# Row maxima eight slots ahead of the exponents in place of ten, in a fused attention and FFN kernel

## The chip, the cores and the metric

The kernel runs on one core of one Trainium2 chip. The metric is device time in microseconds (us), lower is better: before the change the median of 3 runs is 427.05 us (425.29 to 427.09).

## The reference

Input X has 8 batches of 512 rows of 256 numbers, float32. With xn the layernorm of X over the last axis, the result is X + attention(xn) + ffn(xn), float32:

```python
q, k, v = (split_heads(xn @ W.T) for W in (W_q, W_k, W_v))    # 16 heads of 16
q, k = rope(q), rope(k)
scores = causal(einsum("bhqd,bhkd->bhqk", q, k) * 16 ** -0.5) # upper triangle: lowest float
attention = merge_heads(softmax(scores) @ v) @ W_o.T

def fake_quant_fp8(t):                                        # one scale for the whole tensor
    scale = 448 / max(amax(abs(t)), 1e-12)
    return float8_e4m3(t * scale) / scale
ffn = fake_quant_fp8(xn) @ fake_quant_fp8(weight).T + bias
```

The scale of xn needs the largest absolute value of all eight batches.

## The kernel before

**Slots.** The five engines run five programs of their own, tied by semaphores. After a start-up part each program walks through the same numbered slots, from FIRST_SLOT = -LEAD - 1 up to 162. A batch takes 20 slots (SLOTS), 160 for the eight; a slot holds two banks (512 columns each in PSUM) of transposed scores with their exponents, for one fifth of a group of four heads. What is done in a slot is written in tables by hand: an offset per kind of work, relative to 20 times the batch's number. Within a slot each engine's program has a fixed order, and an engine never goes past an instruction that waits.

**Two kinds of scores.** The exponents need each row's maximum beforehand. So the scores are computed twice. `compare` (L989, PE) puts scores into one of three banks s_ps, two banks a slot, and `row_max` (L658, DVE) takes the maxima of each bank's rows. LEAD slots later `attend` (L970, PE) makes the transposed scores in two banks st_ps, with the maximum subtracted, and ACT's exponents (L818) read them. Slots below 0 have `compare` alone, the last LEAD slots of the 160 have `attend` alone. `scores(at, ahead)` interleaves the two, first on PE in each slot. `compare` waits until the bank three before it has been read by DVE, `attend` until the bank two before it has been read by ACT.

**How a maximum becomes a shift.** After ten banks a group's 16 columns of maxima are complete. `turn_max` ("mt", L1058, PE) waits for all of the group's maxima and transposes them into a shared bank; `split_max` (L691, L693, DVE) splits them in two float16 rows, negated; `shift_rows` (L398, SP) sends the two rows into q_st, where they are two more rows of the contraction. The first `attend` of a group waits for that landing.

**The shared banks.** Two PSUM banks, m_ps, serve all the other work of the loop: projections of q and k ("qk", L954, read by DVE's rope, L609 and L610), of V ("v", L1011, read by ACT's copy, L825), transposes of heads ("o", L1018, read by DVE's normalisation, L667 and L671), of two normalised blocks ("at", L1025, read by ACT's copy, L839), outputs ("fin", L1038 and L1046, read by DVE's `finish`, L679), "mt", two steps ("spread") that spread the quantisation's maxima over the partitions, and some filling matmuls ("busy", in five slots). `schedule()` sorts all these by slot, and within a slot by the order of OFFSETS; the bank alternates from item to item. Before each item `bank_free` lets PE wait until the reader of the item two places earlier is done:

```python
at = [i[1:] for i in SHARED].index(item)
if at >= 2:
    kind, n, k = SHARED[at - 2][1:]
    ...
        done, per = reader[kind]
        eng.wait_ge(done, per * n + k + 1)
```

In a slot PE does its scores, then turnings of batches (before slot 0), then the shared items, then PV matmuls (L1080: a first block at slots 3, 8, 13 and 18, the others at 6, 11, 16 and 21). DVE does the slot's two banks of maxima, then `weight_step`, then its part of the shared items in their order, then steps of the quantisation (L755, L759). ACT does its exponents and then copies, among them `copy_heads` (L832) of the first group, in slot 7, which waits for all four "o" of the batch before. In numbers within a batch of 20 slots the loop's items before the change are: 0 fin 1; 1 mt 1; 2 fin 2; 3 o 0; 4 o 1; 5 fin 3; 6 mt 2; 7 o 2, at 0; 8 o 3; 9 v 0; 10 qk 0; 11 mt 3; 12 qk 1; 13 at 1; 14 v 1; 15 qk 2; 16 mt 0 (of the next batch); 17 qk 3; 19 fin 0.

**The prelude.** Batches 0 and 1 are normalised and turned first, batch 0's q and k written to DRAM and read back stacked by heads. In slots -11 to -1 batches 2 to 7 are normalised by ACT (L773), turned by PE (`turn_rows`, L934) into two banks that the exponents and PV use from slot 0 on, and copied by ACT (L797), each at its TURN_SLOT; batch 1 is projected, its rope's result rotated (POOL), cast (ACT, L803) and split (POOL, L349), and V of batch 0 is projected in slots -2 and -1. Statistics of batches 6 and 7 come at slots -LEAD and -LEAD + 3 on DVE. From slot 0 PE waits until all batches are turned.

Of the kernel before, what the change touches and what calls it, by code (L numbers as in the profile page):

```python
# [22 lines left out]
HG = 4  # L23
NG = H // HG
SLOTS = 5 * NG
LEAD = 10
PAIR = 2 * T
SCALE = float(DH) ** -0.5
EPS = 1e-5
# [18 lines left out]
assert BANKS == 2 * SLOTS and ITEMS_UP_TO[-1] == ITEMS  # L48


OFFSETS = {("v", 0): -11, ("v", 1): -6, ("mt", 0): -4, ("mt", 1): 1, ("mt", 2): 6, ("mt", 3): 11,
           ("o", 0): 23, ("o", 1): 24, ("o", 2): 27, ("at", 0): 27, ("o", 3): 28, ("at", 1): 33,
           ("fin", 0): 39, ("fin", 1): 40, ("fin", 2): 42, ("fin", 3): 45,
           ("qk", 0): -30, ("qk", 1): -28, ("qk", 2): -25, ("qk", 3): -23}
LAST_FINS = {("fin", 0): 31, ("fin", 1): 32, ("fin", 2): 34, ("fin", 3): 35}
SPREAD = [(15, "spread", 0, 0), (17, "spread", 0, 1)]
EARLY = {("qk", 1, 0): -LEAD - 1, ("qk", 1, 1): -LEAD - 1, ("qk", 1, 2): -9, ("qk", 1, 3): -8, ("v", 0, 0): -2, ("v", 0, 1): -1}
CHAIN = {("rotate", 0): -27, ("high", 0): -24, ("low", 0): -23, ("write", 0): -21, ("rotate", 1): -21, ("high", 1): -19,
         ("low", 1): -18, ("write", 1): -16, ("read", 0, 0): -19, ("read", 0, 1): -15, ("read", 1, 0): -12,
         ("read", 1, 1): -7}  # L60
EARLY_CHAIN = {("rotate", 0): -10, ("high", 0): -9, ("low", 0): -8, ("write", 0): -7, ("rotate", 1): -7, ("high", 1): -6,
               ("low", 1): -5, ("write", 1): -4, ("read", 0, 0): -5, ("read", 0, 1): -1, ("read", 1, 0): 4,
               ("read", 1, 1): 5}
TURN_SLOT = {2: -10, 3: -8, 4: -7, 5: -6, 6: -4, 7: -3}
BUSY = {slot: 8 for slot in (0, 2, 4, 5, 7)}
LARGEST_SLOT = (0, 2, 4, 5, 7, 8, 9, 11)
DVE_STATS, ACT_STATS = (0, 1, 2, 3, 6, 7), (4, 5)
# [2 lines left out]
def schedule():  # L70


    order = {key: i for i, key in enumerate(OFFSETS)}
    items = [(EARLY.get((kind, n, k), SLOTS * n + (LAST_FINS[kind, k] if (kind, n) == ("fin", NB - 2) else off)),
              order[kind, k], kind, n, k)
             for (kind, k), off in OFFSETS.items() for n in range(NB) if (kind, n) != ("qk", 0)]
    items += [(slot, len(order), kind, n, k) for slot, kind, n, k in SPREAD]
    items += [(slot, len(order), "busy", slot, count) for slot, count in BUSY.items()]
# [4 lines left out]
SHARED_BANK = {item[1:]: i % 2 for i, item in enumerate(SHARED)}  # L83
FIRST_SLOT, END_SLOT = -LEAD - 1, SLOTS * NB + 3

# [9 lines left out]
def exponent_slot(slot):  # L95

    n, s = divmod(slot, SLOTS)
    return (n, s) if 0 <= n < NB else None


def maximum_slot(slot):

    return exponent_slot(slot + LEAD)

# [7 lines left out]
def chain_at(slot, *step):  # L112

    if slot == EARLY_CHAIN[step]:
        return 1
# [36 lines left out]
def attention_ffn_block(nc, x, wq, wk, wv, wo, wf, bias, cos, sin, out):  # L152
    with ExitStack() as ctx:
# [6 lines left out]
        def sem(name):  # L160
            return ctx.enter_context(nc.semaphore(name))
# [126 lines left out]
        wquant = sem("wquant")  # L288
# [168 lines left out]
        def _(eng):  # L457
# [15 lines left out]
            def invert(n):  # L473

                if n in ACT_STATS:
                    i = ACT_STATS.index(n)
                    eng.wait_ge(ln_square, NQ * (i + 1))
                    eng.tensor_scalar(ve[:, n, :], squares[:, i, :], 1.0 / D, EPS, ALU.mult, ALU.add).then_inc(ln_var, 1)
                    eng.wait_ge(ln_var, i + 1)
                else:  # L480
                    eng.wait_ge(ln_ve, 2 * (DVE_STATS.index(n) + 1))
                eng.tensor_tensor(rstd[:, n, :], ve[:, n, :], half[:, :], ALU.pow).then_inc(ln_rstd, 1)
                eng.wait_ge(ln_rstd, 2 * n + 1)
                eng.tensor_tensor(shift_x[:, n, :], nmean[:, n, :], rstd[:, n, :], ALU.mult).then_inc(ln_rstd, 1)  # L484
# [17 lines left out]
            def mask(n, s):  # L502

                u = s % 5
                if u < 2:
                    ap, pat = prob[u].rearrange("p (h q) -> p h q", h=2)[:, :, 0:P], [[0, 2], [1, P]]
                elif u < 4:
                    ap = prob[u].rearrange("p (h q) -> p h q", h=2)[:, :, 0:2 * P]
                    pat = [[0, 2], [0, 2], [1, P]]
                else:  # L510
                    ap, pat = prob[u].rearrange("p (h q) -> p h q", h=4)[:, :, 0:P], [[0, 4], [1, P]]
                eng.wait_ge(exp_done, HALVES * n + 2 * (s + 1))
                eng.sem_inc(mask_begun)
                eng.affine_select(out=ap, in_=ap, compare_op=ALU.is_ge, fill=0.0, base=0,  # L514
                                  pattern=pat, channel_multiplier=-1).then_inc(masked, 1)
# [23 lines left out]
            for slot in range(FIRST_SLOT, END_SLOT):  # L539
# [4 lines left out]
                if at is not None:  # L544
                    mask(*at)
                if slot == -LEAD - 1:
                    invert(4)
                    invert(5)
                if slot == -LEAD + 1:
                    invert(6)  # L550
                if slot == -LEAD + 4:
                    invert(7)
# [26 lines left out]
        def _(eng):  # L579
# [33 lines left out]
            def weight_step(s):  # L613

                nw = NC * D
                if s == 3:
                    eng.wait_ge(w_in, 16 * 4)
                    eng.tensor_reduce(amax[:, NB:NB + 1], wf_sb[:, :, :], AX.XY, ALU.max,
                                      apply_absolute_value=True).then_inc(amax_done, 1)
                if s == 13:  # L620
                    eng.wait_ge(amax_done, NB + 1)
                    eng.tensor_reduce(amax2[:, 0:1], amax[:, 0:NB], AX.X, ALU.max).then_inc(amax_done, 1)
                    eng.tensor_copy(amax2[:, 1:2], amax[:, NB:NB + 1]).then_inc(amax_done, 1)
                if s == 15:
                    eng.wait_ge(full["spread"], 1)
                    eng.tensor_reduce(amax_r[:, :], shared["spread", 0, 0][0:2, 0:P], AX.X, ALU.max).then_inc(wquant, 1)
                    eng.wait_ge(consts, 6)
                    eng.wait_ge(wquant, 1)
                    eng.tensor_tensor(amax_d[:, :], ident[0:2, 0:2], amax_r[:, 0:1].to_broadcast([2, 2]), ALU.mult)\
                       .then_inc(wquant, 1)  # L630
                if s == 17:
                    eng.wait_ge(full["spread"], 2)
                    eng.tensor_scalar(amax_b[:, :], shared["spread", 0, 1][:, 0:2], 1e-12, None, ALU.max)\
                       .then_inc(wquant, 1)
                    eng.wait_ge(wquant, 3)
                    eng.reciprocal(inv[:, :], amax_b[:, :]).then_inc(wquant, 1)
                    eng.tensor_scalar(unscale[:, :], shared["spread", 0, 1][:, 0:2], 1e-12, 1.0 / FP8_MAX, ALU.max, ALU.mult)\
                       .then_inc(wquant, 1)
                if s == 21:
                    eng.wait_ge(wf_scaled, 1)  # L640
                    eng.tensor_scalar(qe[:, 0:nw].bitcast(U32), qv[:, 0:nw].bitcast(U32), 0x7F800000, None,
                                      ALU.bitwise_and).then_inc(qw_exp, 1)
                    eng.wait_ge(qw_exp, 1)
                    eng.tensor_scalar(qe[:, 0:nw], qe[:, 0:nw], 2.0 ** -6, 1.5 * 2.0 ** 20, ALU.max, ALU.mult)\
                       .then_inc(wquant, 1)
# [94 lines left out]
            for slot in range(FIRST_SLOT, END_SLOT):  # L740
                at = maximum_slot(slot)
                if at is not None:
                    n, s = at
# [24 lines left out]
        def _(eng):  # L768
# [42 lines left out]
            def exp(n, s):  # L811
                g, u = divmod(s, 5)
                if n > 0 or g > 0:

                    eng.wait_ge(pv_done, 8 * n + 2 * (g - 1) + (1, 1, 2, 2, 2)[u])
                for half in range(2):
                    eng.wait_ge(st_full, 2 * (SLOTS * n + s) + half + 1)
                    eng.activation(prob[u][:, half * T:(half + 1) * T], st_ps[ST_BANK[2 * s + half]][:, :],  # L818
                                   ACT.Exp, scale=exp_scale[:, 0:1]).then_inc(exp_done, 1)
# [45 lines left out]
            for slot in range(FIRST_SLOT, END_SLOT):  # L865
# [12 lines left out]
                if at is not None:  # L878
                    exp(*at)
                for n in [n for n, at_slot in TURN_SLOT.items() if at_slot == slot]:  # L880
                    copy_turned(n)
# [38 lines left out]
        def _(eng):  # L920
# [172 lines left out]
            def bank_free(item):  # L1093

                kind, n, k = item
                at = [i[1:] for i in SHARED].index(item)
                if at >= 2:
                    kind, n, k = SHARED[at - 2][1:]
                    if kind == "spread":
                        eng.wait_ge(wquant, 1 + 2 * k)  # L1100
                    elif kind != "busy":
                        done, per = reader[kind]
                        eng.wait_ge(done, per * n + k + 1)
                else:
                    eng.wait_ge(roped, at + 1)
# [16 lines left out]
            for slot in range(FIRST_SLOT, END_SLOT):  # L1122
# [3 lines left out]
                scores(exponent_slot(slot), maximum_slot(slot))  # L1126
                for n in [n for n, at_slot in TURN_SLOT.items() if at_slot == slot]:
                    turn_rows(n)
# [61 lines left out]
```

## Time and profile before

| | |
|---|---|
| median of 3 runs | 427.05 us (425.29 to 427.09) |
| the profiled execution | 426.62 us, span 424.9 us |
| PE busy | 383.1 us, 90% of the span, 3034 matmuls |
| DVE busy | 356.4 us, 84% |
| ACT busy | 299.9 us, 71% |
| POOL busy | 247.3 us, 58% |
| mean granted clock of TensorE | 0.972 |
| HBM | 84 GB/s over the span |

Times in the profile's rows are microseconds from the start of the span, means of one instruction are nanoseconds. PE is TensorE's matmul and PEld its weight load, DVE VectorE, ACT ScalarE, POOL GpSimd, SP the engine that issues the transfers. L989 is line 989 of the kernel's file. A row of the timeline gives start, length, engine, line, operation, what is written and read, how many instructions are merged in it, and in brackets the engine's idle time before it with what ended it.

### The profile page before, as it was taken

What the parts mean: (1) busy time and instruction counts of PE and PEld (TensorE: products, weight loads), DVE (VectorE), ACT (ScalarE), POOL (GpSimd) and SP (SyncE); (2) the same over time, 40 slices, a digit from 0 to 9 for tenths busy, and PEclk for the clock granted to TensorE, in tenths of its full rate; (3) what the DMA queues carried; (4) which work ended last, traced back from release to release, by engine and by line L of the source; (5) the groups of instructions that cost most, each with busy time, mean ns of one, the idle gap of its engine ahead of it and who ended that gap; (6) DMA issues with size and microseconds to landing.
All of it is one profiled execution on the core that took longest, in us unless ns stands there. A gap on an engine that the chain in (4) does not pass through costs nothing.

```text
span 424.9 us, 9531 instructions
## 1 busy us (share of the span) xinstructions
PE 383.1 (90%) x3034; PEld 210.4 (50%) x3034; DVE 356.4 (84%) x1358; ACT 299.9 (71%) x507; POOL 247.3 (58%) x270
## 2 busy tenths in 40 slices
PE   7988799988788999899989998999899988896967
PEld 7675466644234545454445444544454443343436
DVE  3888849997889999799979997999799988898203
ACT  3698726665976878777867786778677768777651
POOL 6547402433578767576767567756864665247550
PEclk9998879999899999999999999999999999999988
DMA  7955233000540143314341235124510461101111
GB/s 269 328 156 99 64 89 77 1 3 2 137 117 12 39 134 91 90 39 121 90 104 39 93 97 127 38 59 130 127 39 32 122 161 40 50 2 54 52 50 49
DMA packets 27810, 36.40 MB, mean 86 GB/s; under 512 B 3984, under 2 KB 25872, under 8 KB 26320
## 3 DMA queue, kind: packets, MB, share of 16 engines
q1 hardware_dynamic: 27760, 35.79, 30.9%
q8 instruction: 24, 0.39, 0.4%
q14 instruction: 26, 0.21, 0.2%
HBM read 22.94 MB, written 12.58 MB: 84 GB/s over the span
## 4 chain that ended last, share of the span: by engine, by line
PE 64%; DVE 17%; ACT 8%; issue 8%; POOL 2%; DVEq 0%; ACTq 0%; POOLq 0%
PE o_ps L1080 13%; PE st_ps L970 10%; DVE scratch L658 8%; PE m_ps L1011 7%; PE m_ps L1038 7%; PE m_ps L954 7%; PE s_ps L989 6%; ACT prob L818 6%; DVE prod L610 3%; PE s_ps L926 3%; PE m_ps L926 2%; PE m_ps L1018 2%; PE m_ps L1046 1%; DVE prod L609 1%; PE m_ps L1058 1%
## 5 line engine op out<-in xcount | busy, mean ns | idle before, releaser
L818 ACT ACTIVATE prob<-st_ps,exp_scale 128x512 f32<-128x512 f32 x320 | 204.1, 688 | 81.0 <-PE st_ps L970 79.9
L658 DVE CUSTOM_DVE_ANT_0 scratch<-s_ps,causal 128x512 bf16<-128x512 f32 (+3 forms) x512 | 220.8, 482 | 26.8 <-PE s_ps L989 26.4
L514 POOL TENSOR_SCALAR_AFFINE_SELECT prob<-prob 128x512 f32<-128x512 f32 (+1 forms) x160 | 88.4, 554 | 141.0 <-ACT prob L818 140.2
L989 PE MATMUL s_ps<-k_st,q_st 48*128 48x512 f16 (+3 forms) x512 | 106.5, 303 | 11.1 <-DVE rowmax L658 10.5
L970 PE MATMUL st_ps<-q_st,k_st 50*128 50x128 f16 (+3 forms) x512 | 104.5, 300 | 10.8 <-ACT prob L818 9.1
L1080 PE MATMUL o_ps<-prob,v_sb 128*17 128x512 f32 (+3 forms) x1024 | 82.9, 442 | 7.8 <-ACT heads L832 5.1
L970 PEld LDWEIGHTS st_ps<-q_st,k_st 50*128 50x128 f16 x512 | 33.1, 94 | 88.5 <-ACT prob L818 66.4
L989 PEld LDWEIGHTS s_ps<-k_st,q_st 48*128 48x128 f16 x512 | 33.5, 94 | 27.4 <-DVE rowmax L658 17.7
L658 DVE DVE_READ_ACCUMULATOR2_ANT rowmax<- 128x1 f32 x512 | 40.6, 79 | 0.0
L1080 PEld LDWEIGHTS o_ps<-prob,v_sb 128*17 128x17 f32 x1024 | 23.3, 97 | 32.6 <-issue 19.0
L1011 PE MATMUL m_ps<-wv_sb,xnT 128*128 128x256 f32 x128 | 33.7, 408 | 0.0
L1038 PE MATMUL m_ps<-wo_sb,attnT 128*128 128x256 f32 x116 | 32.6, 403 | 0.0
L349 POOL TENSOR_TENSOR parts<-rot,parts 128x1024 f16<-128x1024 f32 x14 | 29.9, 2139 | 3.2 <-ACT parts L803 3.2
L1011 PEld LDWEIGHTS m_ps<-wv_sb,xnT 128*128 128x128 f32 x128 | 24.1, 198 | 6.8 <-issue 3.9
L832 ACT COPY heads<-o_ps 128x512 f32<-128x512 f32 x32 | 18.9, 590 | 11.2 <-PE m_ps L1018 8.0
L609 DVE SCALAR_TENSOR_TENSOR prod<-m_ps,qk_scale,cos_sb 128x512 f32<-128x512 f32 x30 | 22.3, 742 | 4.2 <-PE m_ps L954 3.2
L954 PE MATMUL m_ps<-x_parts,wk_parts 128*128 128x512 f32 x84 | 24.5, 429 | 0.0
L954 PE MATMUL m_ps<-x_parts,wq_parts 128*128 128x512 f32 x84 | 22.9, 410 | 0.7 <-issue 0.7
L1038 PEld LDWEIGHTS m_ps<-wo_sb,attnT 128*128 128x128 f32 x116 | 19.7, 189 | 7.4 <-issue 5.9
L773 ACT ACTIVATE xnT<-xnT,shift_x,rstd 128x256 f32<-128x256 f32 x32 | 16.5, 592 | 9.3 <-POOL shift_x L484 9.3
L1018 PE MATMUL m_ps<-ident,heads 128*128 128x128 f32 x116 | 19.4, 291 | 3.2 <-DVE attn L671 3.2
L610 DVE SCALAR_TENSOR_TENSOR prod<-m_ps,qk_scale,sin_sb 128x512 f32<-128x512 f32 x30 | 22.1, 736 | 0.0
(125 smaller groups left out, 510.0 us busy)
## 6 DMA issues: line engine op xcount, KB each, us to landing
qk_parts<-parts SPq DMA_DIRECT2D x14, 512.0 KB, 3.1
xnT<-x_dram SPq DMA_DIRECT2D x8, 512.0 KB, 9.0
x_res<-x_dram SPq DMA_DIRECT2D x8, 512.0 KB, 5.1
q_st<-qk_parts SPq DMA_DIRECT2D x15, 256.0 KB, 4.3
k_st<-qk_parts SPq DMA_DIRECT2D x15, 256.0 KB, 3.7
out_dram<-x_res SPq DMA_DIRECT2D x7, 512.0 KB, 3.7
q_st<-qk_parts SPq DMA_DIRECT2D x17, 128.0 KB, 3.8
k_st<-qk_parts SPq DMA_DIRECT2D x17, 128.0 KB, 4.3
```

The source lines that it names most:

```text
L349: eng.tensor_tensor(parts[:, w, 1, a:z, :], rot[:, w, a:z], parts[:, w, 0, a:z, :], ALU.subtract).then_inc(low_done[w], z - a)
L514: eng.affine_select(out=ap, in_=ap, compare_op=ALU.is_ge, fill=0.0, base=0, pattern=pat, channel_multiplier=-1).then_inc(masked, 1)
L610: eng.scalar_tensor_tensor(out=c, in0=bank[:, :], scalar=to_range, in1=sin_sb[:, :], op0=ALU.mult, op1=ALU.mult)\
L658: eng.tensor_tensor_reduce(scratch[:, at % 3, col:col + w], s_ps[at % 3][:, col:col + w], causal[:, T - w:T], 1.0, NEG, ALU.add, ALU.max, ...
L818: eng.activation(prob[u][:, half * T:(half + 1) * T], st_ps[ST_BANK[2 * s + half]][:, :], ACT.Exp, scale=exp_scale[:, 0:1]).then_inc(exp_d ...
L954: mm = eng.matmul(bank[:, :], w_parts[k // 2][:, wp, c, k % 2, :], x_parts[:, xp, c, :], start=(i == 0), stop=(i == len(terms) - 1))
L970: mm = eng.matmul(st_ps[ST_BANK[i]][:, col:col + T - kb * P], k_rows(n, h, ROWS + SHIFT, slice(kb * P, (kb + 1) * P)), q_rows(n, h, ROWS + ...
L989: mm = eng.matmul(s_ps[(BANKS * n + f) % 3][:, col:col + (qb + 1) * P], q_rows(n, h, ROWS, slice(qb * P, (qb + 1) * P)), k_rows(n, h, ROWS ...
L1011: mm = eng.matmul(bank[:, t * D:(t + 1) * D], xnT[:, n, c, (2 * i + t) * P:(2 * i + t + 1) * P], wv_sb[:, c, :], start=(c == 0), stop=(c = ...
L1018: mm = eng.transpose(bank[:, g * P:(g + 1) * P], heads[:, g, qb * P:(qb + 1) * P], ident[:, :])
L1038: mm = eng.matmul(bank[:, 0:D], attnT[:, qb, c, :], wo_sb[:, c, :], start=(first and c == 0), stop=(not first and c == NC - 1))
L1080: mm = eng.matmul(o_ps[32 * i:32 * i + VW, kb * P:T], v_sb[:, n % 2, kb, g * HG + i, :], prob[u][:, col:col + T - kb * P], start=(kb == 0) ...
```

## The change

LEAD goes from 10 to 8, so that the maxima run eight slots ahead of the exponents, and the slots begin at -9. The offsets of "mt" go up by one: the transpose of a group's maxima stands one slot behind the last of them (two before), and three slots ahead of the exponents that use them (four before). The slots of the prelude's work (projections of batch 1, its rotation, cast, split and write, and turnings) are set anew for eight slots. The two steps "spread" move from slots 15 and 17 to 14 and 16, and the bank behind them is held until both readers of the second one are done. SP's slots for the shift rows stay: -3, 2, 7 and 12.

```diff
-LEAD = 10
+LEAD = 8
...
-OFFSETS = {("v", 0): -11, ("v", 1): -6, ("mt", 0): -4, ("mt", 1): 1, ("mt", 2): 6, ("mt", 3): 11,
+OFFSETS = {("v", 0): -11, ("v", 1): -6, ("mt", 0): -3, ("mt", 1): 2, ("mt", 2): 7, ("mt", 3): 12,
...
-SPREAD = [(15, "spread", 0, 0), (17, "spread", 0, 1)]
-EARLY = {("qk", 1, 0): -LEAD - 1, ("qk", 1, 1): -LEAD - 1, ("qk", 1, 2): -9, ("qk", 1, 3): -8, ("v", 0, 0): -2, ("v", 0, 1): -1}
+SPREAD = [(14, "spread", 0, 0), (16, "spread", 0, 1)]
+EARLY = {("qk", 1, 0): -LEAD - 1, ("qk", 1, 1): -LEAD - 1, ("qk", 1, 2): -7, ("qk", 1, 3): -6, ("v", 0, 0): -2, ("v", 0, 1): -1}
...
-EARLY_CHAIN = {("rotate", 0): -10, ("high", 0): -9, ("low", 0): -8, ("write", 0): -7, ("rotate", 1): -7, ("high", 1): -6,
-               ("low", 1): -5, ("write", 1): -4, ("read", 0, 0): -5, ("read", 0, 1): -1, ("read", 1, 0): 4,
-               ("read", 1, 1): 5}
-TURN_SLOT = {2: -10, 3: -8, 4: -7, 5: -6, 6: -4, 7: -3}
+EARLY_CHAIN = {("rotate", 0): -8, ("high", 0): -7, ("low", 0): -6, ("write", 0): -5, ("rotate", 1): -5, ("high", 1): -4,
+               ("low", 1): -3, ("write", 1): -2, ("read", 0, 0): -3, ("read", 0, 1): 1, ("read", 1, 0): 6,
+               ("read", 1, 1): 7}
+TURN_SLOT = {2: -8, 3: -7, 4: -6, 5: -5, 6: -4, 7: -3}
...
-                if s == 15:
+                if s == 14:
...
-                if s == 17:
+                if s == 16:
...
                     if kind == "spread":
-                        eng.wait_ge(wquant, 1 + 2 * k)
+                        eng.wait_ge(wquant, 1 + 4 * k)
```

## Rows read from the trace of the kernel before

**Rows 1.** Table by stage: stretch, its length, busy us of each engine, clock, DMA.
```profile
28.40:61.90 33.50, 28.50 (x121) 18.11 (x121) 25.13 (x105) 22.37 (x47) 16.85 (x20) 0.80 0.42 97
...
217.93:261.54 43.61, 41.43 (x350) 21.42 (x349) 40.40 (x158) 32.91 (x53) 29.47 (x31) 1.00 0.32 86
```

**Rows 2.** Waits: who waited for whom, us in total, times, longest.
```profile
ACT heads L832 <- PE m_ps L1018: 8.0, 7, 1.3
...
PE m_ps L1018 <- DVE attn L671: 3.2, 7, 0.6
```

**Rows 3.** Timeline of PE in the prelude.
```profile
47.98 0.39 PE L989 MATMUL s_ps<-k_st,q_st 48*128 48x128 f16 x2 [1.70 <-DVE rowmax L658]
...
55.75 3.78 PE L1011 MATMUL m_ps<-wv_sb,xnT 128*128 128x256 f32 x8
...
60.00 1.99 PE L1011 MATMUL m_ps<-wv_sb,xnT 128*128 128x256 f32 x8
```

**Rows 4.** Timeline of ACT in the prelude.
```profile
34.79 0.58 ACT L797 COPY xnT<-o_ps 128x512 f32<-128x512 f32 x1
35.27 2.08 ACT L773 ACTIVATE xnT<-xnT,shift_x,rstd 128x256 f32<-128x256 f32 x4
37.45 1.05 ACT L803 CAST parts<-rot 128x1024 f16<-128x1024 f32 x1
...
48.63 2.08 ACT L773 ACTIVATE xnT<-xnT,shift_x,rstd 128x256 f32<-128x256 f32 x4 [0.67 <-POOL shift_x L484]
```

**Rows 5.** Table by stage, the longer stretch at the low clock (the eighth number).
```profile
49.16:59.40 10.24, 10.12 (x33) 6.42 (x33) 5.39 (x26) 4.63 (x9) 2.13 (x1) 0.50 0.32 90
```

**Rows 6.** Timeline of slots 67 and 68 (7 and 8 of a batch).
```profile
212.30 0.27 DVE L691 TENSOR_SCALAR shift<-m_ps 16x128 f16<-16x128 f32 x1
...
212.50 0.38 PE L989 MATMUL s_ps<-k_st,q_st 48*128 48x512 f16 x1
...
212.61 0.28 DVE L693 SCALAR_TENSOR_TENSOR shift<-m_ps,shift 16x128 f16<-16x128 f32 x1
...
213.30 0.60 PE L1025 MATMUL m_ps<-ident,attn 128*128 128x128 f32 x4
...
213.57 0.69 DVE L658 CUSTOM_DVE_ANT_0 scratch<-s_ps,causal 128x512 bf16<-128x512 f32 x1
...
214.47 0.42 DVE L671 TENSOR_TENSOR attn<-m_ps,rden 128x256 f32<-128x256 f32 x1
...
214.95 0.66 PE L1018 MATMUL m_ps<-ident,heads 128*128 128x128 f32 x4 [0.49 <-DVE attn L671]
...
217.32 0.28 PE L970 MATMUL st_ps<-q_st,k_st 50*128 50x256 f16 x1
```

**Rows 7.** Timeline of DVE and of POOL in slot 27.
```profile
126.78 2.88 DVE L759 TENSOR_SCALAR qe<-qe 128x1024 f32<-128x1024 f32 x1
...
126.76 2.36 POOL L499 TENSOR_TENSOR x_parts<-xnT,x_parts 128x1024 fp32r<-128x1024 f32 x1
```

**Rows 8.** Timeline of DVE and of PE in slots 76 to 79.
```profile
236.64 0.08 DVE L658 DVE_READ_ACCUMULATOR2_ANT rowmax<- 128x1 f32 x1
...
238.45 0.73 DVE L609 SCALAR_TENSOR_TENSOR prod<-m_ps,qk_scale,cos_sb 128x512 f32<-128x512 f32 x1
...
236.40 1.66 PE L954 MATMUL m_ps<-x_parts,wk_parts 128*128 128x512 f32 x6
...
240.58 0.28 PE L989 MATMUL s_ps<-k_st,q_st 48*128 48x256 f16 x1 [0.51 <-DVE rowmax L658]
```

**Rows 9.** Timeline of slots 61 and 65; landing of SP's L398 after its issue.
```profile
202.62 0.28 DVE L693 SCALAR_TENSOR_TENSOR shift<-m_ps,shift 16x128 f16<-16x128 f32 x1
...
208.01 0.37 PE L970 MATMUL st_ps<-q_st,k_st 50*128 50x512 f16 x1
...
DMA to landing us min/median/max: 1.6/1.8/4.0
```

**Rows 10.** Timeline of ACT in slot 15.
```profile
98.19 0.59 ACT L825 COPY v_sb<-m_ps 128x512 f32<-128x512 f32 x1
```

## The prediction

> **What bounds the kernel now.** I read, in this order, the table by stage, the waits, and then the timeline of one batch of the loop, engine by engine, and of the prelude. The table by stage shows a loop that repeats: a batch of twenty slots takes 43.61 us, and PE is busy for 41.43 of them and DVE for 40.40 [rows 1]. So the loop has no room: a wait on PE lengthens it unless another wait shrinks by as much. The waits name the place where PE does wait in every batch, slots 7 and 8: PE's turning of the heads (L1018) for DVE's normalised rows, 7 times, and ACT's copy of the heads behind that turning, 7 times [rows 2]. In the prelude PE idles too, for instance 1.70 us for DVE's maxima [rows 3]; it has 28.50 busy us in 33.50 [rows 1].
>
> The sum below is made against the profiled execution: 426.62 us, of which 424.9 are the span. The median of the three runs shown is 427.05, 0.4 above it.
>
> **1. The prelude, two slots shorter.** Work per slot goes up, and what it then follows is ACT's chain of copies and normalisations. A copy pair is two copies of 0.58, about 1.07 together; a normalisation of a batch takes 2.08 [rows 4]. Everything up to the first turning is where it was, and the pair for batch 2 ends at 35.4. From there: normalisation of batch 4 to 37.4, pair 3 to 38.5, normalisation 5 to 40.5, the cast of the rotated rows (1.05) to 41.6, pair 4 to 42.6, normalisation 6 to 44.7, pair 5 to 45.8. Normalisation 7 is held by POOL's shift behind DVE's statistics and starts at 48.63 now; the same eight banks of maxima and the same ropes stand before those statistics in the new order, but the projection that the last rope waits for fell into half clock, which cost some 0.8 (an estimate); so normalisation 7 runs from 47.8 to 49.9, pair 6 to 50.9, and PE's last turning ends at about 51.5. Behind it on PE stand the first transpose of maxima, two slots of comparisons of 0.6 each and V's two projections. At the high clock a projection takes 1.99 [rows 3], which puts slot 0 at 57.0 in place of 61.9: 4.9 gained. At the low clock the turning, the comparisons and the first projection (3.78) cost 3.1 more: slot 0 at 60.1, 1.8 gained. Before, PE's clock was granted at 0.50 (1.2 GHz) from 49.16 to 59.40, after the wait of 1.70 for DVE [rows 3, 5]. In the new order PE waits for normalisation 7 from about 47.5 to 50.4, a longer gap than that one, with less work before it. I take the middle, **-3.4** (-1.8 to -4.9). The Trainium skill (TensorE: Matmul & The Clock Gate, Part 1) says that the throttled clock is the default and that activity releases it. The half-clock row after the waits agrees; by it a denser prelude could keep 2.4 GHz throughout, which is the end at -4.9.
>
> **2. Slot 7: a bank of PSUM.** Shared items take the two banks m_ps in turn, and PE waits before each for the reader of the item two places earlier (`bank_free`). The order of the items in the loop does not change, but the third transpose of maxima, ("mt", 2), moves from slot 6 to slot 7. There the order becomes mt 2, o 2, at 0, so at 0 takes the bank of mt 2 in the same slot, and waits for `split_max` on DVE. DVE does that only after the slot's two banks of maxima. One batch, by [rows 6]: the comparisons end at 212.88 (212.50 + 0.38), DVE's maxima run from there to 214.26 (213.57 + 0.69); `split_max`, 0.58 (212.30 to 212.89 in the old place), would end at 214.83. at 0 (L1025), now at 213.30, starts at 214.88, after mt 2 and o 2 have ended at about 213.7: 1.2 us of new wait on PE. The next slot's comparisons begin 0.53 behind at 0, so at 215.4, and o 3, which starts as they end, at 216.0 in place of 214.95. o 3's old wait for DVE's normalisation (214.47 + 0.42) is swallowed: that now ends at 215.5. Behind o 3 are ACT's copy of the heads, the exponents behind it, PE's first PV block and the next slot's scores (217.32): all 1.03 later. The transpose itself (0.2 us of PE) only changes its slot.
>
> It occurs at slots 27, 47, ... 147, seven times. In the first of these DVE has another wait beside it: its op of 126.78 takes 2.88 us while POOL's split runs from 126.76 to 129.12 [rows 7], and a later start behind `split_max` ends with POOL's all the same. The Trainium skill (SBUF — State Buffer, "SBUF: two separate sides") calls the port pair that these engines share an exclusive lock, the loser fully blocked; the row agrees. There I take 0.3 (0 to 1.0). Six at 1.03 and this one: **+6.5** (+3.4, if only the 0.56 that `split_max` puts ahead of the normalisation counts, to +7.2).
>
> **3. Slots 12 and 17: a projection behind the transpose.** mt 3 now stands before qk 1 in slot 12, mt 0 before qk 3 in slot 17, and each waits for the second bank of the slot before. In slot 17 that bank is done at 236.72 (236.64 + 0.08), so the transpose starts at 236.8 and the projection at 237.0 in place of 236.40; it takes 1.66 and ends at 238.66. DVE would be free for its rope at 238.45 as now [rows 8], since only the order of its own work changes; it waits 0.25. DVE bounds this stretch (PE waits for it at 240.58 [rows 8]), so 0.25 is what the batch pays, though PE's own delay is 0.6. In slot 12 the same working gives 0.2. Five batches at 0.45 (the first, with other waits, is in part 5): **+2.3** (0 to +5, where PE's whole delay of 0.4 and 0.6 counts).
>
> **4. Slots 2 to 6 and the shift rows.** mt 1 moves to slot 2, and its `split_max` stands ahead of DVE's finishing step there. o 0 takes mt 1's bank and waits about 0.1; DVE is 0.2 to 0.5 later up to slot 6. I take 0.15 seven times: **+1.0** (0 to +2.5). The two rows that `split_max` leaves go by SP's transfers into q_st, for the attention five slots on. Of mt 1 they were ready at 202.90 (202.62 + 0.28), and that attention starts at 208.01, 5.1 later [rows 9]. At the new place, behind DVE's maxima of slot 2, they are ready at 205.15, and 2.9 are left. A transfer lands 1.8 us after its issue in the median, 4.0 at worst [rows 9], and two are issued one after the other on SP: enough most times, by little. The other three groups, with a longer stretch of slots before theirs, have 3.4 or more left. SP stands longer at the shift rows, and behind it are the reads of the next stack, which have more than five slots to spare. I take 0 (0 to +2).
>
> **5. The first batch.** The two steps of "spread" come at slots 14 and 16, so the order of banks changes there: qk 2 now takes the bank of v 1 and waits for ACT's copy, which ends at 98.78 (98.19 + 0.59 [rows 10]) where qk 2 began at 97.1. That is 1.7 of PE, most of which the transpose then no longer waits for qk's ropes: **+0.7** (0 to +1.7). The wait 1 + 4k asks for two more tiny DVE instructions, nothing.
>
> **6. The tail.** The maxima are as many as before; two slots' worth moves from the prelude to slots 150 and 151. There PE waits for ACT's exponents, and four banks of comparisons, 0.6 a slot, mostly fit into that: **+0.3** (0 to +1.2).
>
> Sum: 426.6 - 3.4 + 6.5 + 2.3 + 1.0 + 0.7 + 0.3 = **434.0**, 7 above the median.
>
> **Rivals.**
> - A. The bank wait is taken up. For it: PE already waits in slot 8 for the same engine [rows 2]. Against it: both waits stand in one chain, and only one is replaced. If 0.3 a batch remains, the sum is 426.6 - 3.4 + 2.1 + 2.3 + 1.7 = 429.3, or 428 with part 3 smaller.
> - B. Faster: the prelude pays at the high clock, and the loop keeps its 43.6. The mechanism is the clock between 47 and 57 us: if PE's gap before the last turning doesn't lower it, 4.9 are gained, and the change is a gain from the point where the loop's losses stay under 4.9, that is under 0.7 a batch. With 1 us of losses in all the time is 422.7. For it: the half-clock row is the dearest of the prelude. Against it: part 2 alone costs more than 0.7.
> - C. The loop pays more: PE's whole delay in slots 12 and 17 (1.0 a batch, 2.7 more than I take) and shift rows late by 0.5 in most batches (3.0 more) give 439.7. For it: 2.9 us against a transfer of up to 4.0. Against it: DVE's work in that stretch is the same in sum.
>
> **Chances.** Forecast 0.60, A 0.13, B 0.12, C 0.15. About 0.5% (2.1 us) is what a measurement of this kernel can tell from no change: 424.9 to 429.2. Faster takes B, 0.11; same takes most of A and the rest of B, 0.10; slower the rest, 0.79. The range leaves out B and the upper half of C: 427 to 439.
>
> **What would show it.** Right: a batch of about 45 us in the loop; PE's L1025 waits for DVE's L693 by about 1.2 us, seven times less the first; the wait of L1018 for DVE gone; L954 beginning 0.6 later against its slot; slot 0's first scores at 57 to 60. Wrong: a batch still of 43.6 us, L1025 right behind L1018 in slot 7, or a prelude that ends where it did.

## The result, and the profile after

The changed kernel takes 448.05 us (median of 4 runs, 444.11 to 452.03), the kernel before 427.07 beside it: ratio 1.0444, 95% interval 1.0373 to 1.0515. Slower, as forecast, but 14 us above the 434.0 and outside the range. Here and below, ratios and their intervals leave out runs that were disturbed, medians don't. The profiled execution took 446.54 us; its span is 444.8 against 424.9.

Where the 19.9 us between the two spans went, by the first score of chosen slots: slot 0 starts at 62.36 (61.93 before), +0.4. The seven batches from there to slot 140 take 322.1 in place of 307.6, +14.5, of which the four steady ones between slots 40 and 120 give 2.6 each. Slots 140 to 148 give +2.2, slots 148 to 152 +2.8, the rest nothing.

The table by stage of the changed kernel: the prelude, the low-clock stretch in it, a steady batch, and slots 148 to 152 (columns as in [rows 1]).
```profile
28.40:62.36 33.96, 27.64 (x114) 18.26 (x115) 22.37 (x89) 21.84 (x45) 16.87 (x20) 0.75 0.39 94
48.68:62.33 13.65, 11.40 (x31) 7.28 (x31) 4.17 (x20) 5.19 (x10) 2.12 (x1) 0.50 0.35 92
204.38:250.56 46.18, 42.91 (x350) 22.02 (x349) 40.92 (x159) 33.02 (x52) 29.60 (x31) 1.00 0.31 82
...
401.70:414.80 13.10, 11.87 (x68) 4.74 (x67) 7.48 (x30) 7.39 (x11) 4.98 (x6) 0.61 0.13 42
```
Compare the batch with [rows 1], length and PE's busy time together: 46.18 - 43.61 = 2.57 longer, and PE's 350 matmuls are busy for 42.91 in place of 41.43. So 1.48 of the 2.57 is not waiting at all: the same products keep PE longer, at a clock of 1.00. Only the other 1.09 is idle time. The prediction had looked for waits alone, and had left the products at their old durations.

The idle part, from the waits of the changed kernel (PE, then ACT; totals of the whole run, times, longest):
```profile
PE m_ps L1025 <- DVE shift L693: 8.8, 7, 1.3
...
PE m_ps L1058 <- DVE rowmax L658: 2.9, 8, 0.4
...
PE m_ps L954 <- ACT v_sb L825: 1.7, 1, 1.7
```
```profile
ACT heads L832 <- PE m_ps L1018: 4.2, 7, 0.6
```
The first line is the new bank wait, seven times and as long as forecast. L1018's wait for DVE [rows 2] is gone, and ACT's copy of the heads waits 4.2 for L1018 where it waited 8.0 [rows 2]. In the timeline of slots 67 and 68 (PE, then DVE), which answers to [rows 6]:
```profile
221.08 0.66 PE L1025 MATMUL m_ps<-ident,attn 128*128 128x128 f32 x4 [1.30 <-DVE shift L693]
...
222.21 0.66 PE L1018 MATMUL m_ps<-ident,heads 128*128 128x128 f32 x4
223.59 1.05 PE L1080 MATMUL o_ps<-prob,v_sb 128*17 128x512 f32 x8 [0.73 <-ACT heads L832]
```
```profile
220.75 0.28 DVE L693 SCALAR_TENSOR_TENSOR shift<-m_ps,shift 16x128 f16<-16x128 f32 x1
```
`split_max` ends at 221.03 and at 0 starts at 221.08.

The busy part, PE at the start of a batch, the scores of slot 60 and the next work, first before and then after the change:
```profile
198.58 0.39 PE L970 MATMUL st_ps<-q_st,k_st 50*128 50x512 f16 x1
198.58 0.39 PE L989 MATMUL s_ps<-k_st,q_st 48*128 48x512 f16 x1
198.80 0.38 PE L970 MATMUL st_ps<-q_st,k_st 50*128 50x512 f16 x1
198.81 0.38 PE L989 MATMUL s_ps<-k_st,q_st 48*128 48x128 f16 x2
199.12 1.13 PE L1038 MATMUL m_ps<-wo_sb,attnT 128*128 128x256 f32 x4
```
```profile
204.38 0.39 PE L970 MATMUL st_ps<-q_st,k_st 50*128 50x512 f16 x1
204.60 0.38 PE L989 MATMUL s_ps<-k_st,q_st 48*128 48x128 f16 x2
204.82 0.38 PE L970 MATMUL st_ps<-q_st,k_st 50*128 50x512 f16 x1
205.04 0.38 PE L989 MATMUL s_ps<-k_st,q_st 48*128 48x512 f16 x1
205.35 1.13 PE L1038 MATMUL m_ps<-wo_sb,attnT 128*128 128x256 f32 x4
```
Before, a score (L970, 50 rows) and a comparison (L989, 48 rows) start at the same time, and the slot's four take 0.54 us to the next work. After, each starts about 0.22 behind the one before it, and the four take 0.97. Heads 0 to 7 lie in partitions 0 to 63, heads 8 to 15 in 64 to 127. Five slots hold a group of four heads, so maxima ten slots ahead belong to the group two further on, always in the other half; eight slots ahead, in slots 0, 1, 10 and 11 of a batch, they belong to the next group, in the same half. The Trainium skill (TensorEngine Tiling (Array Packing), Tiling Modes) says that tiles of the array run independently, and that a tile is tied to its partitions; the two fences agree with it.

The prelude, PE behind the wait for the last normalisation:
```profile
50.93 1.09 PE L934 MATMUL st_ps<-ident,xnT 128*128 128x128 f32 x4 [2.96 <-ACT xnT L797]
...
53.98 3.78 PE L1011 MATMUL m_ps<-wv_sb,xnT 128*128 128x256 f32 x8
57.69 1.03 PE L989 MATMUL s_ps<-k_st,q_st 48*128 48x256 f16 x3
58.65 3.78 PE L1011 MATMUL m_ps<-wv_sb,xnT 128*128 128x256 f32 x8
62.36 0.39 PE L970 MATMUL st_ps<-q_st,k_st 50*128 50x512 f16 x1
```
The last turning begins at 50.93, about where the prediction had it, and from there on everything runs at the granted clock of 0.50: both projections take 3.78, where before one of them had 1.99 [rows 3].

### The profile page after: what moved, and what is told of

Same layout as the page of the kernel before. It is cut to its first block, busy times and chain, and to the rows that moved or that the text cites. A ratio compares the mean times of both kernels' runs of the same rounds, so it can differ in the third digit from the quotient of the medians.

```text
span 444.8 us, 9531 instructions
## 1 busy us (share of the span) xinstructions
PE 397.3 (89%) x3034; PEld 216.4 (49%) x3034; DVE 358.5 (81%) x1358; ACT 300.3 (68%) x507; POOL 247.2 (56%) x270
## 4 chain that ended last, share of the span: by engine, by line
PE 65%; DVE 15%; ACT 9%; issue 8%; POOL 1%; DMA 1%; DVEq 0%; SPq 0%; ACTq 0%; POOLq 0%
PE o_ps L1080 13%; PE st_ps L970 11%; PE m_ps L1011 8%; PE m_ps L954 7%; PE s_ps L989 7%; DVE scratch L658 6%; PE m_ps L1038 6%; ACT prob L818 5%; PE m_ps L926 2%; PE m_ps L1018 2%; PE m_ps L1025 2%; DVE prod L610 2%; PE s_ps L926 2%; DVE prod L609 1%; ACT heads L832 1%
## 5 line engine op out<-in xcount | busy, mean ns | idle before, releaser
L970 PE MATMUL st_ps<-q_st,k_st 50*128 50x128 f16 (+3 forms) x512 | 109.0, 303 | 9.4 <-ACT prob L818 6.8
L989 PE MATMUL s_ps<-k_st,q_st 48*128 48x512 f16 (+3 forms) x512 | 110.6, 305 | 5.8 <-DVE rowmax L658 5.0
L970 PEld LDWEIGHTS st_ps<-q_st,k_st 50*128 50x128 f16 x512 | 36.0, 94 | 89.3 <-ACT prob L818 52.2
L989 PEld LDWEIGHTS s_ps<-k_st,q_st 48*128 48x128 f16 x512 | 38.1, 95 | 25.3 <-DVE rowmax L658 13.0
L1011 PE MATMUL m_ps<-wv_sb,xnT 128*128 128x256 f32 x128 | 35.5, 425 | 0.0
L1011 PEld LDWEIGHTS m_ps<-wv_sb,xnT 128*128 128x128 f32 x128 | 25.2, 207 | 7.3 <-issue 4.0
L954 PE MATMUL m_ps<-x_parts,wk_parts 128*128 128x512 f32 x84 | 23.9, 422 | 1.7 <-ACT v_sb L825 1.7
L954 PE MATMUL m_ps<-x_parts,wq_parts 128*128 128x512 f32 x84 | 22.7, 407 | 0.7 <-issue 0.7
L1018 PE MATMUL m_ps<-ident,heads 128*128 128x128 f32 x116 | 19.5, 293 | 0.7
```

Of the source, the lines that this page charges most:

```text
L954: mm = eng.matmul(bank[:, :], w_parts[k // 2][:, wp, c, k % 2, :], x_parts[:, xp, c, :], start=(i == 0), stop=(i == len(terms) - 1))
L970: mm = eng.matmul(st_ps[ST_BANK[i]][:, col:col + T - kb * P], k_rows(n, h, ROWS + SHIFT, slice(kb * P, (kb + 1) * P)), q_rows(n, h, ROWS + ...
L989: mm = eng.matmul(s_ps[(BANKS * n + f) % 3][:, col:col + (qb + 1) * P], q_rows(n, h, ROWS, slice(qb * P, (qb + 1) * P)), k_rows(n, h, ROWS ...
L1011: mm = eng.matmul(bank[:, t * D:(t + 1) * D], xnT[:, n, c, (2 * i + t) * P:(2 * i + t + 1) * P], wv_sb[:, c, :], start=(c == 0), stop=(c = ...
L1018: mm = eng.transpose(bank[:, g * P:(g + 1) * P], heads[:, g, qb * P:(qb + 1) * P], ident[:, :])
```

## The experiments

Batches are read from the profiled runs, in stretches where the clock was 1.00 unless another is named. Theory: the 2.57 a batch is the bank wait, the halves, and the projections of slots 12 and 17; where the prelude ends is set by the clock.

**1. The bank wait taken away** from the changed kernel.
```
-OFFSETS = {("v", 0): -11, ("v", 1): -6, ("mt", 0): -3, ("mt", 1): 2, ("mt", 2): 7, ("mt", 3): 12,
+OFFSETS = {("v", 0): -11, ("v", 1): -6, ("mt", 0): -3, ("mt", 1): 2, ("mt", 2): 8, ("mt", 3): 12,
```


> The changed kernel with the third transpose of maxima in slot 8 of a batch in place of slot 7, so that the turning at 0 no longer takes its bank in the same slot. Bank theory: PE's wait of L1025 for split_max is gone, a batch of the loop goes from 46.18 to about 45.2 us, the whole about 6 to 7 us below the changed kernel. Rival (maxima that run only eight slots ahead leave DVE too late, wherever the transpose stands): the batch stays at 46.2, the wait only changes its name.

440.01 us (436.86 to 442.59), ratio 1.0276 (1.0192 to 1.036). A steady batch:
```profile
201.23:246.46 45.23, 42.81 (x350) 22.07 (x349) 40.83 (x159) 32.86 (x52) 29.52 (x31) 1.00 0.31 83
```
0.95 less a batch, 0.85 of it idle time (46.18 - 42.91 = 3.27 before this edit, 45.23 - 42.81 = 2.42 with it): the longer busy time stays, as it must if it is something else. The prelude's code is the same, yet slot 0 starts at 59.43 in place of 62.36, since the low clock held from 47.0 to 57.2 only.

**2. Opposite halves again** in the changed kernel: the comparisons of slots 0, 1, 10 and 11 read the head eight further on (these maxima then belong to other heads), with the wait for its rows.
```
+                    if f == 16:
+                        eng.wait_ge(stack_in[1], HALF_STACK * (n + 1))
...
+                if f // 2 in (8, 9, 18, 19):
+                    h = (h + HH) % H
```


> The changed kernel, but in slots 0, 1, 10 and 11 of a batch compare reads eight heads further, from the other 64 partitions (the maxima of these heads are wrong, the sizes the same). Row-half theory (the two kinds of scores run beside each other in PE's array only where their operands lie in opposite halves of the partitions): the slots' scores take 0.61 us in place of 1.04, a batch goes from 46.18 to about 44.9, the whole 9 us down. Rival (the pairing of bank sizes, or DVE, makes these slots long): no change.

441.23 us (440.22 to 447.81), ratio 1.03 (1.0227 to 1.0372). A batch:
```profile
206.58:251.65 45.07, 41.37 (x349) 21.28 (x348) 40.79 (x159) 32.87 (x52) 29.53 (x31) 1.00 0.32 84
```
1.1 less a batch, and here it is the busy time that falls, by 1.54 to 41.37, as low as before [rows 1]; 0.43 of that comes back as idle time (3.70 in place of 3.27). The sizes of the products are the same as in the changed kernel, so the sizes don't make the difference.

**3. The same cost put into the kernel before**, lead of ten.
```
+                if f // 2 in (10, 11):
+                    h = (h + HH) % H
```


> The kernel before, lead of ten, with one thing changed: in slots 0 and 1 of every batch the comparisons take the head eight further on, whose rows lie in the same half of the array as those of the scores being made beside them (the maxima of these two slots belong to other heads, so the output is not the reference's). Row-half theory: two products of 64 rows run side by side only in opposite halves; the two slots that now lie in one half cost what slots 0 and 1 cost after the change, 0.43 + 0.24 us, so a batch goes from 43.6 to about 44.3 us and the time by +5 (427 to 432, eight batches), with the scores of those slots ending one behind another. Rival (the halves don't matter, the 0.67 us was the half clock or the shift rows): batch 43.6, time 427.

432.25 us (428.64 to 437.58), ratio 1.0094 (1.0059 to 1.0129). The batch, and PE at its start (L991 is L989 in this run):
```profile
196.38:240.66 44.28, 42.11 (x349) 21.89 (x348) 40.57 (x160) 33.01 (x52) 29.43 (x31) 1.00 0.32 85
```
```profile
196.40 0.39 PE L970 MATMUL st_ps<-q_st,k_st 50*128 50x512 f16 x1
196.63 0.38 PE L991 MATMUL s_ps<-k_st,q_st 48*128 48x512 f16 x1
196.85 0.38 PE L970 MATMUL st_ps<-q_st,k_st 50*128 50x512 f16 x1
197.07 0.38 PE L991 MATMUL s_ps<-k_st,q_st 48*128 48x128 f16 x2
```
0.67 a batch over [rows 1] for two slots, and the staircase of 0.22 comes with it. The halves are shown from both sides.

**4. The bank wait put into the kernel before**, by moving the transposings one slot later with the lead kept at ten.
```
-OFFSETS = {("v", 0): -11, ("v", 1): -6, ("mt", 0): -4, ("mt", 1): 1, ("mt", 2): 6, ("mt", 3): 11,
+OFFSETS = {("v", 0): -11, ("v", 1): -6, ("mt", 0): -3, ("mt", 1): 2, ("mt", 2): 7, ("mt", 3): 12,
...
-SPREAD = [(15, "spread", 0, 0), (17, "spread", 0, 1)]
+SPREAD = [(14, "spread", 0, 0), (16, "spread", 0, 1)]
...
```


> The kernel before (ten slots ahead) with the transposes of maxima one slot later and spread in slots 14 and 16, as the change has them, and nothing else. Bank theory: the wait of L1025 for split_max appears 7 times, a batch goes from 43.62 to about 44.6, the whole to about 433. Rival (the eight slots' lead makes the wait): 427, since the maxima are complete two slots before the transpose.

437.57 us (436.33 to 440.41), ratio 1.0234 (1.0151 to 1.0318).
```profile
PE m_ps L1025 <- DVE shift L693: 8.8, 7, 1.3
```
```profile
199.00:243.22 44.22, 40.85 (x351) 21.16 (x350) 40.18 (x159) 32.90 (x52) 29.49 (x31) 1.00 0.32 85
```
The same wait, to the tenth, with the old lead: it comes from the slot of the transposing alone. It nets 0.6 a batch here, since other slots shrink by about 0.4. The time is above the 433 expected: the clock fell in two later batches (261 to 268 and 309 to 312), which took 47.2 and 45.8.

**5. The clock in the prelude**: products without use put into PE's idle time of the changed kernel (7 before the third turning, 12 in slot -3, 24 before the last turning).
```
+                if slot in {-3: (12, ("mt", 0, 0))}:
...
+                    if n in {3: (7, ("qk", 1, 2)), 7: (24, ("mt", 0, 0))}:
+                        count, item = {3: (7, ("qk", 1, 2)), 7: (24, ("mt", 0, 0))}[n]
+                        bank_free(item)
+                        keep_busy(count, shared[item])
```


> The changed kernel with filling matmuls in PE's waits of the prelude: 7 before batch 3's turning, 12 ahead of slot -3, 24 before batch 7's turning. Clock theory: the granted clock stays at 1.00 to slot 0, V's two projections take 1.99 each in place of 3.78, slot 0 begins at about 57.5 in place of 62.4, the whole 4 to 5 us down. Rival (ACT's chain or DVE bounds the prelude, whatever the clock): slot 0 stays at 61 to 62.

449.06 us (446.27 to 455.29), ratio 1.0469 (1.037 to 1.0568), where 4 to 5 less than the changed kernel was expected. PE before slot 0, and a batch of the profiled run (the slowest of the four):
```profile
48.87 5.63 PE L926 MATMUL m_ps<-ident 128*128 128x128 f32 x48
...
55.94 2.00 PE L1011 MATMUL m_ps<-wv_sb,xnT 128*128 128x256 f32 x8
...
58.41 2.00 PE L1011 MATMUL m_ps<-wv_sb,xnT 128*128 128x256 f32 x8
60.33 0.39 PE L970 MATMUL st_ps<-q_st,k_st 50*128 50x512 f16 x1
```
```profile
205.46:253.25 47.79, 44.52 (x350) 22.50 (x349) 40.92 (x159) 32.98 (x52) 29.53 (x31) 0.96 0.30 78
```
The clock stayed at 1.00 and the projections take 2.00, but the 24 fillers are 48 records, twice the time meant, and the last turning starts behind them at 54.33, 3.4 later than without. In the loop, batches take 47.8 with a fall of the clock in each. The run says that the prelude's clock can be held, not what that is worth.

**6. The same with fewer.**
```
-                if slot in {-3: (12, ("mt", 0, 0))}:
+                if slot in {-3: (6, ("mt", 0, 0))}:
...
-                    if n in {3: (7, ("qk", 1, 2)), 7: (24, ("mt", 0, 0))}:
+                    if n in {3: (3, ("qk", 1, 2)), 7: (9, ("mt", 0, 0))}:
```


> The changed kernel with fillers of half the count of the first filled run (3 before the third turning, 6 in slot -3, 9 before the seventh turning). Clock theory: the clock stays at full speed in the prelude and nothing waits for the fill, slot 0 starts at about 57 (the prediction's value for the full clock) in place of 62.4, and the time falls by 5 to about 443 if the loop keeps its batches of 46.2. Rival (the two slots less are taken back by the turnings' chain whatever the clock): slot 0 at 60 or later, as in the first filled run. If the loop's clock drops come in every batch, as in that run, batches of 47.8 and a time of 450 follow with slot 0 at 57 all the same.

449.97 us (437.94 to 452.95), ratio 1.0273 (1.0209 to 1.0337). The prelude, one batch, and the next:
```profile
28.40:57.36 28.96, 26.54 (x151) 19.67 (x151) 22.28 (x90) 21.92 (x46) 16.84 (x20) 0.94 0.34 81
204.82:250.98 46.16, 42.89 (x350) 22.03 (x349) 40.88 (x159) 33.01 (x52) 29.55 (x31) 1.00 0.31 82
250.98:298.60 47.62, 44.35 (x350) 22.41 (x349) 40.90 (x159) 33.01 (x52) 29.55 (x31) 0.96 0.30 79
```
Slot 0 at 57.36: the clock theory's 57, and the prediction's value for the full clock (57.0). The two quickest of the six runs took 437.94 and 442.17, at mean clocks of 0.988 and 0.965. But in the profiled run, the slowest, the clock falls in most batches of the loop, for instance from 270.0 to 273.4, where PE waits in slots 7 and 8:
```profile
267.68 0.66 PE L1025 MATMUL m_ps<-ident,attn 128*128 128x128 f32 x4 [1.30 <-DVE shift L693]
...
270.20 1.91 PE L1080 MATMUL o_ps<-prob,v_sb 128*17 128x512 f32 x8 [0.73 <-ACT heads L832]
```
PV's first block takes 1.91 there and 1.05 in the changed kernel's profile. A batch with such a fall is 1.5 longer than its neighbour. Over all profiles, each fall between slots 40 and 120 (experiments 4, 5 and 6) begins in slot 8 of a batch, at the second of these two waits, and none of the seven profiles without the wait of L1025 for DVE's L693 has a fall there. The profiles of the changed kernel and of experiment 2 have the wait and no fall there. So the wait may cost more than its own length; that it brings the fall isn't shown. The changed kernel's own four runs, at mean clocks of 0.943 to 0.965, spread over 8 us where the kernel before spread over 4; that fits, but only one of them has a trace.

**7. All three undone together** in the changed kernel: the edits of 1, 2 and 6.
```
+OFFSETS = {("v", 0): -11, ("v", 1): -6, ("mt", 0): -3, ("mt", 1): 2, ("mt", 2): 8, ("mt", 3): 12,
...
+                if f // 2 in (8, 9, 18, 19):
+                    h = (h + HH) % H
...
+                if slot in {-3: (6, ("mt", 0, 0))}:
...
+                    if n in {3: (3, ("qk", 1, 2)), 7: (9, ("mt", 0, 0))}:
...
```


> The changed kernel, lead of eight, with the three prices taken off together: the third transposing of the maxima one slot later (bank wait), the comparisons of slots 0, 1, 10 and 11 of a batch on heads of the other half (their maxima belong to other heads, so the output is not the reference's), and the short fillers in the prelude. If the terms are separate and add up: batch 46.2 - 0.95 - 1.1 = 44.1 to 44.2 us, of which 0.5 over the kernel before is left to the projections of slots 12 and 17; slot 0 at 57.4; the time about 427, 424 to 431 by where the clock falls: the kernel before's own. Rival (the terms overlap, or a cause is still missing, as a later shift of rows): batch 45 or more and 433 or more.

430.34 us (426.86 to 432.3), ratio 1.0049 (1.0012 to 1.0085).
```profile
28.40:57.22 28.82, 26.34 (x150) 19.51 (x150) 22.18 (x88) 21.79 (x45) 16.86 (x20) 0.94 0.37 80
197.83:241.98 44.15, 41.30 (x349) 21.25 (x349) 40.70 (x159) 32.80 (x52) 29.57 (x31) 1.00 0.33 86
```
The batch is 44.15, the sum's 44.1 to 44.2, and slot 0 is at 57.22. In a steady batch the terms are separate. What is left over [rows 1] is 0.54 a batch: slots 12 and 17 take 0.62 and 0.75 longer than before, and the other slots 0.83 less. In both slots PE waits for DVE's maxima before the transposing (L1062 here):
```profile
224.07 0.27 PE L1062 MATMUL m_ps<-ident,rowmax 128*16 128x128 f32 x1 [0.39 <-DVE rowmax L658]
...
236.52 0.27 PE L1062 MATMUL m_ps<-ident,rowmax 128*16 128x128 f32 x1 [0.39 <-DVE rowmax L658]
```
Slot 0 comes 4.7 earlier than in the kernel before, yet the span is 3.0 longer (427.9 against 424.9): beside the 0.54 of the steady batches, the first two give back 3.3 (48.21 and 48.14 for 46.08 and 46.95, with the clock down three times in them where it was once), and slots 148 to 152 another 3.4 (13.76 for 10.33).

**8. The late transposing by itself**, in the kernel before, one slot behind its maxima.
```
-OFFSETS = {("v", 0): -11, ("v", 1): -6, ("mt", 0): -4, ("mt", 1): 1, ("mt", 2): 6, ("mt", 3): 11,
+OFFSETS = {("v", 0): -11, ("v", 1): -6, ("mt", 0): -5, ("mt", 1): 0, ("mt", 2): 5, ("mt", 3): 10,
...
```


> The kernel before, lead of ten, with the transposings of the maxima one slot earlier (slots 0, 5, 10 and 15 of a batch in place of 1, 6, 11 and 16; the two spreads from slots 15 and 17 to 14 and 16), so that each stands one slot behind its last maxima, as after the change, ahead of a projection in slots 10 and 15; halves, banks of the heads and lead stay. Theory of the late maxima: the projection behind them waits for the previous slot's maxima, 0.2 to 0.45 in each of the two slots: batch 43.6 to 44.1 or 44.5, time 430 to 434. Rival (the distance to the maxima costs nothing, and what was left over in the changed loop is the shift rows' three slots): batch 43.6, time 427.

442.92 us (442.25 to 443.75), ratio 1.0359 (1.0323 to 1.0395): far over either value. The waits show why it can't decide:
```profile
PE m_ps L954 <- ACT v_sb L825: 12.4, 11, 1.5
...
PE m_ps L1058 <- DVE rowmax L658: 2.7, 7, 0.4
```
With the transposing a slot earlier, the order of the banks changes again, and projections (L954) get the bank that ACT's copy of v holds, 12.4 us in all. It is another bank wait of the kind of part 2; the price of slots 12 and 17 isn't isolated by it.

**9 and 10. A faster version sought**: the kernel before with two turnings of the heads one slot earlier, and then with 15 fillers in the prelude as well.
```
-           ("o", 0): 23, ("o", 1): 24, ("o", 2): 27, ("at", 0): 27, ("o", 3): 28, ("at", 1): 33,
+           ("o", 0): 23, ("o", 1): 24, ("o", 2): 26, ("at", 0): 27, ("o", 3): 27, ("at", 1): 33,
...
+                if slot in {-8: (8, ("qk", 1, 3)), -5: (7, ("mt", 0, 0))}:
...
```


> The kernel before with the third and fourth turning of the heads one slot earlier (from slots 7 and 8 of a batch to 6 and 7). Bank theory: in the kernel before the turning in slot 7 waits for its bank, 3.2 us over 7 batches, and the heads' copies start late behind it; one slot earlier the bank's reader has been over for longer in slot 6, while slot 7's turning then stands where the second result did, so a batch loses 0.5 to 1.1 us: 42.5 to 43.1, time 419 to 423. Rival (the wait only moves: the earlier turning asks for a bank that is read just as late, or for rows of the heads that aren't there yet): batch 43.6 to 44.2, time 427 to 431.

> The turnings one slot earlier as in the run beside it, and 15 small products without use put into PE's two longest idle stretches of the prelude (8 in slot -8, 7 in slot -5), each about 0.23 us long. Clock theory: with PE kept at work the clock stays at full speed through the prelude, the projections take 2.0 us in place of 3.8 each, and slot 0 starts at about 58 in place of 61.9: 3 to 4 us less than the run beside it. Rival (the prelude is bound by ACT's casts and the turnings' wait for them, at either clock): slot 0 at 60.5 or later, the same time as the run beside it within 1.5 us.

425.94 us (425.24 to 430.41), ratio 0.9965 (0.9934 to 0.9995), and 425.75 us (422.77 to 426.08), ratio 0.992 (0.9888 to 0.9952): both less than 1% below the kernel before. The second one's prelude and batch, and PE's last turning:
```profile
28.40:56.74 28.34, 25.40 (x151) 17.65 (x150) 24.67 (x101) 21.96 (x45) 16.84 (x20) 1.00 0.42 104
195.90:239.10 43.20, 41.45 (x350) 21.43 (x348) 40.39 (x161) 32.78 (x52) 29.51 (x31) 1.00 0.33 87
```
```profile
50.82 0.63 PE L934 MATMUL st_ps<-ident,xnT 128*128 128x128 f32 x4 [0.93 <-ACT xnT L797]
```
A batch loses 0.41, less than the 0.5 to 1.1 expected. Slot 0, at 56.74, comes 4.7 earlier than in the profile without fillers, and the first batch gives 1.6 of that back (47.70 against 46.09), with the clock down from 96.2 to 99.6. Of the 3 to 4 us expected of the fillers the medians show 0.2. And this is the prelude of ten slots: with the clock held it starts slot 0 as early as that of eight (57.36 and 57.22).

## Why the prediction was right in its direction and wrong in its size

The forecast of the profiled run was 434.0, it took 446.5: 12.5 missing. An estimate puts 7.5 of that on the halves (seven batches at 1.07, the step from experiment 1's 45.22 to experiment 7's 44.15); 3.8 are the prelude (+0.4 for -3.4) and 2.5 slots 148 to 152 (+2.8 for the tail's +0.3). What remains, -1.3, is a difference: the batches outside the steady stretch grew by less.

- **Part 2, the bank wait, was right.** 1.03 a batch was forecast, and its removal gives 0.95. PE's wait was put at 1.2 and is 1.3 at its longest. Experiment 4 shows it with the old lead. Rival A, that it is taken up, fell (its sum of 429.3 also leaves out the tail's 0.3).
- **The failing step is the sum for a batch in parts 2 to 4**: it follows waits and leaves every product its old duration, so that a lost overlap stands in it at nothing. In its place the runs show 1.48 more busy time of PE in a steady batch, worth 1.07 to 1.11 of its length (experiments 2 and 7). The head that stands beside a comparison changes with the lead; that PE does two products at once was in the trace before (198.58, twice), and no step asked whether it would stay so.
- **Part 1, the prelude: ACT's chain was right, the clock and what was put down to the two slots were not.** The last turning was expected from about 50.4 and starts at 50.93. The two ends were 57.0 at the high clock and 60.1 at the low one; the low end let only the turning, the comparisons and the first projection be slow, and the clock stayed at 0.50 to 62.33, over both. With the clock mostly held, 57.36 and 57.22 are measured for the 57.0. But the 4.9 of that end compares a prelude at the high clock with one that had lain at 0.50 for 10.24 us [rows 5]. With ten slots and the clock held, slot 0 starts at 56.74 (experiment 10), and the last turning waits for the same copy of ACT, to 50.82 there and to 50.93 after the change. So the 4.9 is the clock's, and no run shows a gain from the two slots at the full clock. That the idle gap alone brought the clock down isn't shown.
- **Part 3, slots 12 and 17**: 0.45 a batch was forecast, and with part 4's 0.15 that is 0.60 against the 0.54 left in experiment 7. The size fits, and the wait of 0.39 is in the trace of experiment 7 in both slots, but the split is another, and so the fit is partly luck: slot 19 is 0.42 shorter and gives most of slot 17's back, and slot 12's stays, where the prediction let DVE take up part of both.
- **Part 4, the shift rows**: 0 was forecast and PE waits for that transfer once, for 0.5:
```profile
PE st_ps L970 <- DMA q_st<-shift: 0.5, 1, 0.5
```
  With the third transposing a slot later still (experiment 1), it is 4.3 over four waits: the reserve was as thin as the prediction said.
- **Part 5, the first batch**: the wait of L954 for the copy of v is the forecast 1.7.
- **Part 6, the tail**: slots 148 to 152 take 13.10 in place of 10.33, at a mean clock of 0.61, since it is at 0.50 from 403.7 on; before, it fell only behind them, at 411.0. In the changed kernel that fall too begins in slot 8 of a batch (148), at the second of the two waits (403.64). But neither the lead nor the wait of L1025 is needed for a fall there: in experiment 8, with ten and without that wait, the same slots take 12.95 at 0.78, and in experiment 7 13.76. What moves it stays open.
- **Rivals B and C** fell: the steady batch is 46.18 and not B's 43.6. C came nearer in size, 439.7 for 446.5, but by another mechanism: the shift rows are late once, by 0.5.

## What to carry to other kernels

When a lead or an offset changes, ask of every pair of products that run side by side whether they still lie in different halves of the array; a table by stage tells the loss by PE's busy time, not by a wait. A shared pair of banks ties items to the reader two places back, so an item that moves by one slot gives another item a new wait, and the order has to be written out for each trial. Where the granted clock differs from run to run, price a stretch at both levels to its very end, for the kernel before and the one after alike, and make the range hold both: else the clock's part is put down to the change.

## What the runs showed of the hardware

- The same prelude code started slot 0 at 62.36 and at 59.43 (the changed kernel and experiment 1), and with the old prelude at 61.93 and 58.34 (before and experiment 3), as the mean granted clock from 28.4 us on was 0.75 and 0.83, 0.80 and 0.89. So two profiles of one prelude differed by about 3 us.
- The four products of a slot's scores and comparisons (50 and 48 rows) take 0.54 us when the two kinds lie in opposite halves of the partitions (slot 60 before) and 0.97 when they lie in the same one (slot 60 after).
- A float32 filler of 128 columns is two records, about 0.23 us together at the full clock (48 records in 5.63 us).
- The same two waits of slots 7 and 8, 1.30 and 0.73, came with a fall of the clock in some batches (47.62) and without one in others of the same run (46.16).
- Slot 0 started at 56.74 with ten slots of prelude at a granted clock of 1.00 (experiment 10) and at 57.22 with eight at 0.94 (experiment 7).
